# The last tile of a feed is a maxima tile, the rows of maxima leave from ScalarE's queue, and a group's first loads move into a batch's first block

## The reference

```python
bias = where(one of the 3 columns with the largest band_importance, -inf, 0)
q, k, v = x @ Wq.T + bq, x @ Wk.T + bk, x @ Wv.T + bv          # 16 heads x 32
attn = softmax(q @ k.T / sqrt(32) + bias)                       # per head, 2048 x 2048
y = layernorm(x + (attn @ v) @ Wo.T + bo) * gamma + beta
x1 = layernorm(x + y)
h = x1 @ hadamard(512)
q4 = clip(round(h / s), -8, 7) * s,  s = max|h| / 7 per token
out = layernorm(x1 + q4 @ ternary(w_ffn).T)
```

## Time and profile before

| | |
|---|---|
| median of three runs | 4854.95 us |
| the profiled execution, its own time | 4854.98 us |
| its span (first to last instruction) | 4853.2 us |
| mean granted TensorE clock | 0.983 of full speed |
| TensorE matmul busy | 4667.6 us, 96% |
| GpSimd busy | 3642.9 us, 75% |
| VectorE busy | 3318.9 us, 68% |
| ScalarE busy | 2596.1 us, 53% |

### The profile page before, as it was taken

One profiled execution on the slowest core, in us unless ns is written; L12 is line 12 of the kernel. 1 busy time (PEld: TensorE's weight loads), 2 busy tenths in 40 slices (PEclk: granted clock), 3 DMA queues, 4 the chain that ended last, 5 costly groups with the idle time before them and its releaser, 6 DMA issues.

```text
span 4853.2 us, 83960 instructions
## 1 busy us (share of the span) xinstructions
PE 4667.6 (96%) x24152; PEld 2375.4 (49%) x24152; DVE 3318.9 (68%) x5886; ACT 2596.1 (53%) x4891; POOL 3642.9 (75%) x1215
## 2 busy tenths in 40 slices
PE   7999999999899999999989999999999999999987
PEld 4445545554544555554454454555545444554434
DVE  3776676666777666666767767666676776667637
ACT  1455555554555555555455555555545655555545
POOL 1687777887488887777748877788875888877885
PEclk8899999999999999999999999999999999999998
DMA  9113232324411333322441223333334123332112
GB/s 207 32 40 71 58 72 63 70 66 105 127 40 43 66 70 69 75 62 64 114 112 41 56 60 71 67 66 67 76 112 99 50 48 66 70 68 59 29 53 72
DMA packets 245915, 346.30 MB, mean 71 GB/s; under 512 B 14801, under 2 KB 100561, under 8 KB 245458
## 3 DMA queue, kind: packets, MB, share of 16 engines
q1 hardware_dynamic: 245458, 340.73, 29.6%
HBM read 205.33 MB, written 33.55 MB: 49 GB/s over the span
## 4 chain that ended last, share of the span: by engine, by line
PE 78%; POOL 7%; DMA 6%; issue 4%; DVE 2%; ACT 1%; SPq 1%; POOLq 0%; ACTq 0%; DVEq 0%
PE ps_m L544 25%; PE ps_s L559 19%; PE ps_o L585 15%; PE ps_z L564 5%; DMA qst<-lo 5%; PE ps_z L531 4%; PE ps_m L505 3%; PE ps_z L499 3%; POOL acc L1117 3%; POOL prob L1143 1%; POOL prob L1147 1%; PE ps_s L505 1%; POOL prob L1132 1%; PE ps_s L499 1%; POOL prob L1126 1%
## 5 line engine op out<-in xcount | busy, mean ns | idle before, releaser
L926 DVE TENSOR_REDUCE umax<-ps_m 128x1 f32<-128x512 f32 x4096 | 2497.1, 681 | 757.7 <-PE ps_m L544 757.7
L1117 POOL TENSOR_TENSOR acc<-acc,prob 128x2048 f32<-128x2048 f32 x624 | 2858.2, 4580 | 151.2 <-ACT prob L783 101.7
L783 ACT ACTIVATE prob<-ps_s 128x512 f32<-128x512 f32 x4096 | 2131.5, 609 | 940.9 <-PE ps_s L559 927.1
L544 PE MATMUL ps_m<-kst,qst 97*128 97x512 f32 x4096 | 1872.0, 460 | 57.6 <-DMA qst<-lo 36.9
L559 PE MATMUL ps_s<-qst,kst 99*128 99x512 f32 x4096 | 1635.5, 400 | 12.2 <-ACT prob L783 9.9
L544 PEld LDWEIGHTS ps_m<-kst,qst 97*128 97x128 f32 x4096 | 777.7, 190 | 996.0 <-DVE umax L926 738.0
L585 PE MATMUL ps_o<-prob,vst 128*32 128x512 f32 x8192 | 976.7, 600 | 0.0
L559 PEld LDWEIGHTS ps_s<-qst,kst 99*128 99x128 f32 x4096 | 780.2, 191 | 138.9 <-ACT prob L783 31.5
L1117 POOL TENSOR_TENSOR acc<-prob 128x2048 f32<-128x2048 f32 x64 | 291.1, 4548 | 401.2 <-ACT prob L783 401.2
L585 PEld LDWEIGHTS ps_o<-prob,vst 128*32 128x32 f32 x8192 | 228.0, 110 | 530.8 <-issue 331.1
L1101 POOL TENSOR_TENSOR obuf<-obuf,zinv 128x512 f32<-128x512 f32 x64 | 82.4, 1287 | 442.1 <-ACT obuf L810 442.1
(11 more groups left out here) (114 smaller groups left out, 2528.8 us busy)
## 6 DMA issues: line engine op xcount, KB each, us to landing
xk<-in_xT_dram SPq DMA_DIRECT2D x66, 1024.0 KB, 8.6
xq<-in_xT_dram SPq DMA_DIRECT2D x65, 1024.0 KB, 5.8
kst<-hi SPq DMA_DIRECT2D x128, 256.0 KB, 6.8
qst<-hi SPq DMA_DIRECT2D x128, 256.0 KB, 5.2
wq<-in_wT_dram SPq DMA_DIRECT2D x65, 256.0 KB, 6.1
kst<-lo SPq DMA_DIRECT2D x64, 256.0 KB, 5.6
qst<-lo SPq DMA_DIRECT2D x64, 256.0 KB, 3.9
ctxT_dram<-obuf SPq DMA_DIRECT2D x64, 256.0 KB, 2.4
```

The source lines that it names most:

```text
L544: nc.tensor.matmul(ps_m[:, u % NMB, :], qst[k % 2][0:RSTACK, h, qt * P:(qt + 1) * P], kst[k // NQB % 2][0:RSTACK, h, kb * QB:(kb + 1) * QB ...
L783: nc.scalar.activation(prob[:, c % NPB, h, :], ps_s[:, (i * HG * NKC + HG * c + h) % NSB, :], ACT.Exp, scale=SCALE).then_inc(ex, 1)
L926: nc.vector.tensor_reduce(umax[:, m, kb:kb + 1], ps_m[:, u % NMB, :], AX.X, ALU.max).then_inc(mred, 1)
L1117: nc.gpsimd.tensor_tensor(acc[:], a, prob[:, c % NPB], ALU.add).then_inc(padd, 1)
```

## The change

- `FEED` gives the order of a feed: m0 s0 m1 s1 m2 s2 m3 s3 m4 s4 s5 m5 s6 m6 s7 m7. Until s4 nothing moves; s5, s6 and s7 each stand one place earlier and m5, m6 and m7 one place later, so that m7 is the feed's last tile.
- `maxima` leaves SyncE's queue. ScalarE issues that DMA itself, behind its own copy to `mrow` and a wait for that copy. SyncE's `low_queries` then stands right behind `queries`.
- `maxima_to_rows` moves ahead of the column sums of chunk 15.
- `next_stage` leaves `keys` and the token phase. It is called once behind the first `keys`, and then in block 0 of every batch, behind `next_queries`.

```diff
--- before.py
+++ after.py
@@ -40,6 +40,7 @@
 UP = UNITS // NP
 QUARTER_PAIR = 2
 VALUE_BANK = NMB - 1
+FEED = "msmsmsmsmssmsmsm"
 LATE_SUMS = NKC - 4
 NT = L // P
 LN1, LN2, LN3 = range(3)
@@ -324,7 +325,6 @@
 
                 for t in range(NQB):
                     keys_quarter(stage, b, s, t)
-                next_stage(stage, b, s)
 
             def next_stage(stage, b, s):
                 for t in range(2):
@@ -348,12 +348,6 @@
             def next_queries(b, k):
                 load_x(xq[:], batch_of(b, k + 1), (k + 1) % NQB).then_inc(xq_ld, 16)
                 load_w(wq[:], 0, (k + 1) // NQB % NG).then_inc(wq_ld, 16)
-
-            def maxima(f, k):
-
-                sp.wait_ge(mcp, f + 1)
-                both = qst[k % 2][RM0:RM0 + 2].rearrange("p h (q x) -> p (h q) x", x=P)
-                sp.dma_start(both.bitcast(F32), mrow[:].bitcast(F32)).then_inc(q_cur, 16)
 
             def store_context(n, i, stage):
                 wait_alone(sp, cbias, n + 2, passed)
@@ -418,8 +412,6 @@
                             store(bb, s - AGE[LN3])
                         if not last and 0 < s - KEY_STEP <= NQB:
                             keys_quarter(bb * NG + NG + 1, bb, NG + 1, s - KEY_STEP - 1)
-                if not last:
-                    next_stage(b * NG + NG + 1, b, NG + 1)
 
             sp.dma_start(rows[0:1, 8:10, :], band.rearrange("a (b n) -> a b n", b=2)).then_inc(band_ld, 16)
             sp.dma_start(bias[:], bqkv).then_inc(bias_ld, 16)
@@ -435,6 +427,7 @@
             for k in range(NST):
                 sp.sem_inc(c_st[k], 16)
             keys(0, 0, 0)
+            next_stage(0, 0, 0)
             sp.wait_ge(stk_ones, 4)
             sp.wait_ge(mask_ok, 2)
             for par in range(2):
@@ -448,7 +441,6 @@
             queries(1, 1)
             low_queries(1, 1)
             next_queries(0, 1)
-            maxima(0, 0)
 
             def batch(b, last):
                 for i in range(NBLK):
@@ -457,6 +449,8 @@
                         if not (last and i >= NBLK - 2):
                             wait_alone(sp, qproj, n + 3, passed)
                             next_queries((n >> 4) & (NB - 1), i + 2)
+                        if i == 0:
+                            next_stage((n >> 2) + 1, (n >> 4) & (NB - 1), 1)
                         if projects(i, last):
                             block_quarter((n >> 2) + 1, (n >> 4) & (NB - 1), s + 1, i % NQB)
                         if i == NBLK - 1:
@@ -466,9 +460,6 @@
                         wait_alone(sp, sc, (n + 1) * (HG * NKC), passed)
                         if not (last and i >= NBLK - 2):
                             queries(n + 2, i + 2)
-                        if not (last and i == NBLK - 1):
-                            maxima(n + 1, i + 1)
-                        if not (last and i >= NBLK - 2):
                             low_queries(n + 2, i + 2)
                         if i == NBLK - 1:
                             load_second_tile((n >> 4) & (NB - 1), last)
@@ -566,14 +557,18 @@
 
             def feed(n, i, p, last):
 
-                for c in (2 * p, 2 * p + 1):
-                    for h in range(HG):
-                        u = HG * c + h
+                k, u = UP * p, UP * p
+                for what in FEED:
+                    if what == "s":
+                        c, h = divmod(k, HG)
+                        score(n, i, c, h, head=i == 0 and c == 0)
+                        k += 1
+                    else:
                         if projects(i, last) and p == QUARTER_PAIR + 1 and u < UP * p + NMB and u % NMB == VALUE_BANK:
                             pe.wait_ge(v_cp, (n >> 2) * NQB + (NQB + i % NQB + 1))
                         if not (last and i == NBLK - 1):
                             unit(u, n + 1, i + 1, (n >> 2) + 1 if i % NQB == NQB - 1 else None)
-                        score(n, i, c, h, head=i == 0 and c == 0)
+                        u += 1
 
             def context(n, i, p):
 
@@ -616,10 +611,10 @@
                         pe.wait_ge(mred, (n + 1) * UNITS + UP * (p + 1))
                         values_of(i % NQB, ps_m[:, VALUE_BANK, :])
                 for c in pe_sums(i):
+                    if c == NKC - 1 and not (last and i == NBLK - 1):
+                        maxima_to_rows(n + 1)
                     if c >= LATE_SUMS:
                         chunk_sums(n, i, c)
-                if not (last and i == NBLK - 1):
-                    maxima_to_rows(n + 1)
                 pe.wait_ge(padd, added(n, i) + additions(i))
                 column_sums(acc, False, True).then_inc(zdone, 1)
                 context(n, i, NP - 2)
@@ -767,9 +762,12 @@
                 act.wait_ge(qproj, f + 1)
                 nc.scalar.activation(hi[:, 0], bank, ACT.Identity, bias=bias_of(0, k // NQB)).then_inc(q_hi, 1)
 
-            def maxima_rows(f):
+            def maxima_rows(f, k):
                 act.wait_ge(mtr, f + 1)
                 nc.scalar.activation(mrow[:], ps_m[0:2 * HG * NQB, 1, 0:P], ACT.Copy).then_inc(mcp, 1)
+                both = qst[k % 2][RM0:RM0 + 2].rearrange("p h (q x) -> p (h q) x", x=P)
+                act.wait_ge(mcp, f + 1)
+                act.dma_start(both.bitcast(F32), mrow[:].bitcast(F32)).then_inc(q_cur, 16)
 
             def exponential(n, i, c, h):
 
@@ -804,7 +802,7 @@
                         keys_of(stage + 1, i // NQB + 1, t, ps_z[:, :], 1)
                         values_of(stage + 1, i // NQB + 1, t, ps_m[:, VALUE_BANK, :])
                 if not (last and i == NBLK - 1):
-                    maxima_rows(n + 1)
+                    maxima_rows(n + 1, i + 1)
                 act.wait_ge(pv, n * NKC + 2 * NKC)
                 act.wait_ge(cst, (n + 1) * 16)
                 nc.scalar.activation(obuf[:], ps_o[:], ACT.Copy).then_inc(oz_cp, 1)
@@ -868,7 +866,7 @@
             keys(1, 1, 1)
             act.wait_ge(k_stk[0], 2 * (2 * NSTK))
             queries(1, 1, ps_m[:, 0, :])
-            maxima_rows(0)
+            maxima_rows(0, 0)
             def batch(b, last):
                 for i in range(NBLK):
                     with block_of(act, b, i) as n:
```

## The result

The changed kernel takes 4735.47 us (median of four runs, 4731.28 to 4739.79) against 4855.13 us (4854.8 to 4862.21) for the kernel before: a ratio of 0.975, 95% interval 0.9733 to 0.9767. The forecast was 4733 us, the range 4700 to 4790. Two of its terms were off in opposite directions, and they are the better part of the lesson.

A forecast was written before the change was run, and what follows sets the result against it. TensorE (78% of the span) was taken as the bound, paced by VectorE in a feed's second half, plus the qst<-lo transfer (5%). 77.5 + 41 + 0 + 1 + 4, less 1, gave 122 us: 4855 to 4733, range 4700 to 4790.

The forecast's parts named there:

- Part 1: Order of the feed: m0 to context 4.17 us instead of 4.34, 77.5 us gained in all, ends 0 and about 103.
- I take 0.165, which all rows of this feed support: Steady feed: gain of 0.165 us per feed, 1.32 us a block, chosen between bounds of 0 and 0.235.
- the rival's figure, 0.235: Feed: s5 does not wait because exponentials come a little earlier, 0.235 us gained per feed; total 4707 us, chance 0.15.
- The kind 0 to 3: 16 early blocks without projection: GpSimd's additions limit the gain to 1.17 us each, 18.7 us in all.
- the rival with the falling clock: Early blocks: GpSimd becomes the bound and the clock falls, 4773 us; chance 0.08 together with the no-effect stack case.
- Part 2: Block ends: with the maxima off SyncE's queue, m0's wait for qst<-lo goes in 57 blocks, 41 us gained.
- the maxima arrive late: ScalarE's queue: maxima land late beside the stacks, s0 waits 3.5 us in 60 blocks, 4943 us; chance 0.04.
- Part 3: Transpose ahead of chunk 15: same matmuls moved around, maxima rows leave 0.86 us earlier, gain 0.
- Part 4: Group's loads in block 0: cost 0, and 1 us gained in all at the turns between batches.
- The 4 us of the token phase: Token phase's second tile: its 1.51 us wait for a context load goes in three batches, 4 us gained.
- Last four blocks: Last batch's last four blocks, already waiting 4.34 us for GpSimd: only the additions' earlier start gained, 0.7 us.
- The two large terms: The order of the feed, 77.5 us, and the wait for qst<-lo at block ends, 41 us.

The follow-up runs named there:

- the run with the waits reordered: Changed kernel with ScalarE's wait for the score written behind the two buffer waits at each chunk's first exponential: 4706.89 us, ratio 0.9695.
- The queue's part alone: Kernel before with only the DMA of the maxima issued by ScalarE, SyncE's wait for the copy gone too: 4818.6 us, ratio 0.9929.
- the transpose put back: Changed kernel with the transpose of the maxima back behind the column sums of chunk 15: 4740.7 us, ratio 0.9765.
- the run that keeps the wait: Kernel before with ScalarE sending the maxima, but SyncE still waiting for the copy ahead of qst<-lo: 4821.41 us, ratio 0.993.
- the feed alone: Kernel before with the new order of the feed and nothing else: 4774.06 us, ratio 0.9838.
- the run with the loads alone: Kernel before with the group's first loads moved into block 0 and nothing else: 4856.75 us, ratio 1.0002.

## Why the prediction was right, and where it was wrong

**Part 1, the feed: right, with an error of 0.03 us in the step that mattered.** The prediction placed s5's load at 2.56, m5 at 2.90, m7 at 3.84 and the context at 4.17; measured 2.55, 2.89, 3.87 and 4.19, median 4.20. It had only s5 wait, and the fifth exponential past before s7; in fact s5, s6 and s7 each load 0.06 us behind the exponential that they need, and the pairs of tiles behind s5 come at ScalarE's 0.49 us instead of 0.47. The 0.14 us of a median feed make 1.12 a block, and the loops gained 1.10 (forecast 1.32). The step that failed is "I take 0.165, which all rows of this feed support": all those rows came from a feed in a loop, and the last batch, written out, has another ScalarE program. There the rival's figure, 0.235, came true (1.88 us a block = 8 x 0.235). The reason named for that rival, an exponential somewhat earlier (0.15 us), was the right one, and the run with the waits reordered shows it in the loops too; that s5 would then not wait was not, the rows have 0.22 us.

**The kind 0 to 3: right.** -17.8 against -18.7 us. Blocks last 56.9 to 57.2 us (a batch's first block left out), forecast 56.9 to 57.1, and GpSimd's last addition ends 0.05 to 0.3 us ahead of the sums; in the last batch their first matmul waits 0.7 us for it (forecast up to 0.2). Nothing of the rival with the falling clock shows there. Projecting blocks last 63.1 to 63.5 us in loops (forecast 63.0 to 63.2) and 62.4 in the last batch.

**Part 2, the wait for the stack: right in size (41 forecast, 41.8 measured), wrong on the margin and on the cause.** The prediction had the stack land at most 6.8 us after the first, 3 us behind the sums, 1.4 us before m0 is due. It lands 6.8 us after its *own* issue and 8.0 after the issue of the first, 4.2 us behind the sums (690.48 - 686.29), 0.2 us before m0's load. Its argument that being issued 3 us earlier is more than the 0.66 needed is the step at fault: landing did not follow the issue. (It also took the hi stacks to be issued 3.8 and 1.9 us before the sums; the trace before has 3.6 and 3.0, which changes little.) The queue's part alone brought 36.7 us, with m0 still right behind the landing; the other 5 came only in the company of the rest (40.5 with the transpose put back), where the feed's last score, and with it the stacks, stands 0.26 us earlier. That m0 was due just behind the landing is luck. And the run that keeps the wait shows that the wait on `mcp` was not what cost: the small DMA in front of the stack was.

**The rival *the maxima arrive late* did not occur.** s0 never waited for mrow, except in the first block, where it waited before as well. ScalarE's issue (0.66 us in the rows above) lay in idle time, as said.

**Part 3: right in the change, not by itself.** "It moves the same matmuls around, so TensorE's own sum is 0" is true of TensorE. Alone, the step brings 18 us through the DMA that it releases earlier, which the prediction never counted because part 2 had already taken that wait.

**Part 4: 1 us for the turn was 0** (turns to batches 1 and 2 idle 8.31 and 8.22 us after, 8.28 and 8.25 before). **The 4 us of the token phase were wrong in sign.** The prediction let the 1.51 us wait of the second tile go, because SyncE would issue its load earlier, behind an earlier stack. The same place after:

```profile
1140.46 4.54 PE L634 MATMUL ps_s<-vst,hi 128*128 128x512 f32 x6 [2.19 <-DMA hi<-ctxT_dram]
...
1146.56 2.74 PE L634 MATMUL ps_s<-vst,hi 128*128 128x512 f32 x6
...
1140.46:1144.84 4.38, 4.38 (x7) 1.84 (x8) 2.58 (x5) 0.00 (x0) 2.79 (x3) 0.61 0.57 169
1146.56:1150.85 4.29, 4.29 (x12) 1.90 (x11) 3.41 (x11) 0.86 (x2) 2.56 (x2) 1.00 0.40 122
```

At a batch's end other loads stand in front of the hi stacks on SyncE's queue. The stack is issued 0.81 us behind the sums (1.27 before) and lands where it landed, at 7.62 (7.61), so SyncE's loads of the tile stand where they stood, from 7.9 us behind the sums on. The wait became 2.19 us, and the six matmuls behind it took 4.54 us at a granted clock of 0.61; the next tile's took 2.74 at 1.00. The step "with the stack earlier that goes" is the one that failed, and the parts alone show why. With the queue alone the three waits for the second tile fell from 1.51, 1.60 and 1.19 us to 0.61, 0.37 and 1.21, half of what was forecast. With the feed alone they grew to 1.99, 2.39 and 1.84: measured from the sums, SyncE comes to the stacks later (the first hi stack 0.48 us ahead instead of 1.23 at the first batch's end). In the changed kernel they are 2.19, 1.60 and 2.56. The four stretches from a batch's last sums onward changed by +2.3, -1.8, +3.8 and +2.0 us. What decides the rest of these is not settled; the run with the loads alone has +2.7, -3.8 and +0.4 at the first three, so part of it is scatter.

**Last four blocks: mis-sized, 5.6 us for 0.7.** Only the start of the additions was counted, and that came out: from m0 to sums these blocks gained 0.75 us. The other 4.9 lie in the three stretches from sums to m0, which took 6.13 us (clock 0.72), 4.43 and 4.43, before 6.94 (0.63), 7.10 and 5.81. The waits at the sums fell from 4.34 to 3.98 in block 12 and from 4.35 to 2.40 in block 13, but shorter waits need not explain more than about half: with the queue moved and its wait kept the waits are as before, 4.34, 4.35 and 2.64, and the stretches took 6.13, 6.82 and 4.43. What sets the clock there otherwise stays open. The prediction had the price of a wait at the lower clock, 2.5 us, in its rival, and used it only as a danger, not as something that could be won back.

Summed: the feed came out 4 us short of the forecast (72.4 for 76.8 before the last four blocks), the token phase 11 short, the last blocks and the time ahead of the first block 7 better. The total lies within 3 us of the median and 7 of the profiled execution (4739.79 us). The two large terms were each right in size; that the small ones nearly cancel is luck.

## What to carry to other kernels

Where one engine alternates between two consumers, put the tile whose consumer is ahead next to last and read, from the rows of one feed, both the old wait and the one that takes its place; then read the same rows in every written-out copy of the loop, since its waits may be placed otherwise. A small DMA in front of a large one on the critical path costs about its issue time each time (0.62 to 0.74 us here); move it to an idle engine's queue. Do not carry a landing time from a lone transfer to a packed one: here the last of three landed 8.0 us behind the issue of the first, once it was itself issued soon enough. Let the wait that comes last in time stand on the working instruction itself. In this kernel that takes writing it last in the loop and first in the written-out copy, so look at the instructions of both.

## What the runs showed of the hardware that was not expected

- **A wait in front of a register instruction starts the work later.** ScalarE's first exponential of a feed starts 0.92 us behind m0 when the wait for the score sits on a register instruction ahead of the exponential, 0.77 when it sits on the exponential itself: 0.15 us, which is on the path only where a score waits for ScalarE. The trace has the two instructions in between at 603.59 and 603.66, ahead of the exponential at 603.74. In the written-out batch one such instruction in between makes 0.86 of 0.77. In this kernel the 0.15 us are 29 us of 4735.
- **An earlier issue can mean a longer landing.** The same 256 KB stack takes 3.9 us from issue to landing when issued 1.14 us behind the sums, 4.1 at 0.40, 4.5 at 0.25 with the small DMA just in front, and 6.8 when issued right behind the two hi stacks. Issued 3.75 us earlier with respect to the sums in the changed kernel, it landed 0.9 us earlier. In three of the kernels it lands 8.0 us behind the issue of the first of the three stacks, though it is issued 1.3 us behind that one in two of them and 4.0 in the third.
- **A wait of some microseconds can cost more than itself.** Behind waits of 4.34, 3.98 and 2.19 us the next stretch ran at granted clocks of 0.63, 0.72 and 0.61, part of it at the lower of the two levels, 1.2 GHz; behind a wait of 0.67 it ran at 1.00. The length of the wait alone does not decide: behind 4.34 us the stretch from sums to m0 took 6.94 us before and 6.13 with the queue moved and its wait kept, behind 2.65 and 2.64 us (block 14) 5.81 and 4.43, its time at full clock. In block 12 of the changed kernel's last batch the lower clock cost 1.7 us (6.13 against 4.43) on top of the wait.
